# Layout of SBUF behind the value phase, Wq in a buffer of its own, and K's evacuation earlier in the step, in an attention and ternary-FFN kernel

## The reference

```python
q, k, v = proj(x, Wq), proj(x, Wk), proj(x, Wv)          # y = x @ W.T, split in 16 heads
scores = einsum('bhqd,bhkd->bhqk', q * min(cond, 4), k) / sqrt(64)
attn = softmax(where(causal, scores, min_float))
y = einsum('bhqk,bhkd->bhqd', attn, v) -> (8, 512, 1024) @ Wo.T
q_w = clip(round(w / alpha), -1, 1) * alpha               # alpha = mean |w|
q_x = clip(round(y / s), -128, 127) * s                   # s = row maximum / 127
out = x + q_x @ q_w.T + bias
```

## Time and profile before

| | |
|---|---|
| median of 3 runs | 2042.46 us (2041.6 to 2043.03) |
| profiled execution | 2044.32 us, its span 2042.3 us |
| granted TensorE clock, mean | 0.987 of full speed |
| TensorE / weight loads busy | 95% / 83% |
| VectorE / ScalarE / GpSimd busy | 66% / 50% / 45% |
| moved by DMA | 477.83 MB, mean 234 GB/s |
| chain that ended last | PE 82%, DVE 7%, DMA 4%, issue 3%, ACT 2%, POOL 2% |

### The profile page before, as it was taken

The page is one execution under the profiler, slowest core; times in us unless marked ns, Lnnn a source line. Parts: engine busy times, 40 slices in busy tenths (PEclk is TensorE's granted clock), DMA queues, the critical chain, the costliest instruction groups (busy, mean ns, idle before and its releaser), DMA issues.

```text
span 2042.3 us, 40256 instructions
## 1 busy us (share of the span) xinstructions
PE 1935.3 (95%) x12347; PEld 1697.0 (83%) x12378; DVE 1357.6 (66%) x3330; ACT 1027.5 (50%) x2495; POOL 916.2 (45%) x985
## 2 busy tenths in 40 slices
PE   8999889899998999998999999999988999999998
PEld 6788667899998999998999988999976777777775
DVE  6545665477778777788777787777777545454554
ACT  4443333377677776777777777777774000000000
POOL 1333443344446444465444455444454544444441
PEclk9999989899999999999999999999999999999999
DMA  6899998877777867777778777786772332323332
GB/s 216 327 374 350 343 344 313 300 270 242 271 267 264 284 246 269 275 254 260 274 261 287 233 273 261 256 286 236 277 242 76 118 110 92 123 92 116 100 101 73
DMA packets 165696, 477.83 MB, mean 234 GB/s; under 512 B 12768, under 2 KB 84448, under 8 KB 135776
## 3 DMA queue, kind: packets, MB, share of 16 engines
q1 hardware_dynamic: 165072, 476.11, 66.5%
q10 hardware_dynamic: 528, 0.52, 0.1%
HBM read 331.88 MB, written 111.15 MB: 217 GB/s over the span
## 4 chain that ended last, share of the span: by engine, by line
PE 82%; DVE 7%; DMA 4%; issue 3%; ACT 2%; POOL 2%; SPq 0%; DVEq 0%; ACTq 0%; POOLq 0%
PE proj_ps L211 26%; PE s_ps L598 9%; PE proj_ps L598 8%; PE o_ps L377 7%; PE t_ps L339 6%; PE t_ps L1012 6%; PE o_ps L669 5%; PE o_ps L1012 4%; PE s_ps L299 3%; PE s_ps L300 3%; DMA xv_raw<-xT 2%; DVE pt_all L363 2%; DMA parts<-x_scratch 2%; DVE prob L311 1%; DVE xv L910 1%
## 5 line engine op out<-in xcount | busy, mean ns | idle before, releaser
L211 PE MATMUL proj_ps<-parts 128*128 128x256 f32 x5376 | 770.2, 291 | 15.2 <-DMA parts<-x_scratch 10.0
L211 PEld LDWEIGHTS proj_ps<-parts 128*128 128x128 f32 x5376 | 678.5, 192 | 27.3 <-issue 10.5
L329 POOL TENSOR_TENSOR prob<-prob,row_inv 128x128 f32<-128x128 f32 (+3 forms) x512 | 376.9, 736 | 597.6 <-DVE row_inv L323 597.2
L317 ACT ACTIVATE prob<-prob,row_min 128x128 f32<-128x128 f32 (+3 forms) x512 | 287.6, 562 | 175.1 <-DVE row_min L311 167.8
L363 DVE TENSOR_TENSOR pt_all<-t_ps,pt_all 128x128 fp32r<-128x128 f32 (+3 forms) x512 | 249.4, 487 | 108.0 <-ACT pt_all L356 106.8
L339 PE MATMUL t_ps<-ident,prob 128*128 128x128 f32 x1280 | 229.3, 277 | 49.4 <-DVE pt_all L363 42.0
L311 DVE CUSTOM_DVE_ANT_0 prob<-s_ps,mask 128x128 f32<-128x128 f32 (+3 forms) x512 | 247.8, 484 | 34.1 <-PE s_ps L300 6.9
L654 ACT ACTIVATE yt_q<-t_ps 128x1024 bf16<-128x1024 bf16 x32 | 32.8, 1024 | 426.6 <-PE t_ps L647 426.6
L356 ACT ACTIVATE pt_all<-t_ps 128x128 fp32r<-128x128 f32 (+3 forms) x512 | 217.1, 424 | 8.5 <-PE t_ps L339 6.1
L339 PEld LDWEIGHTS t_ps<-ident,prob 128*128 128x128 f32 x1280 | 153.2, 142 | 72.4 <-issue 47.7
L598 PE MATMUL proj_ps<-wo_parts,o_parts 128*128 128x512 f32 x768 | 187.5, 398 | 0.0
(11 more groups left out here) (126 smaller groups left out, 2824.2 us busy)
## 6 DMA issues: line engine op xcount, KB each, us to landing
parts<-x_scratch SPq DMA_DIRECT2D x224, 1024.0 KB, 7.9
x_scratch<-xv SPq DMA_DIRECT2D x112, 512.0 KB, 5.9
k_sw<-k_st SPq DMA_DIRECT2D x128, 256.0 KB, 3.7
xv_raw<-xT SPq DMA_DIRECT2D x17, 1024.0 KB, 8.8
v_scratch<-v_tmp SPq DMA_DIRECT2D x64, 256.0 KB, 5.3
v_raw<-v_scratch SPq DMA_DIRECT2D x32, 512.0 KB, 3.9
oT_scratch<-o_sum SPq DMA_DIRECT2D x64, 256.0 KB, 2.6
o_raw<-oT_scratch SPq DMA_DIRECT2D x32, 512.0 KB, 4.6
```

The lines of the kernel that those rows point to most:

```text
L211: mm = pe.matmul(qk_bank(w, m), wc[w][:, c, wp, k, :], xq[:, c, :, xp, k, :], start=(fresh and k == 0 and i == 0), stop=(k == CH - 1 and i ...
L317: act.activation(prob[u % QT], prob[u % QT], ACT.Exp, bias=row_min[:, u % 4:u % 4 + 1], scale=-1.0, accum_out=row_sum[:, u % 4:u % 4 + 1]) ...
L329: pool.tensor_tensor(prob[u % QT], prob[u % QT], row_inv[:, u % 4:u % 4 + 1].broadcast_to([P, w]), ALU.mult).then_inc(norm_done, 1)
```

## The change

Five things are changed, and the arithmetic stays the same.

1. `parts` is laid out as x, Q's weights, K's weights instead of K, x, Q. Parts of x of batch 0 therefore lie on value weights that are free earlier in the last pair, K's weights on those that are free last. The buffers of the last phase and of the attention phase are put in another order.
2. The first Wq gets a buffer of its own, `w_first`, and is loaded in pair 2, right behind the first Wk. All later weights use `w_raw` as before.
3. In the last pair, SP issues all parts of x of batch 0 in the first four places. ScalarE and VectorE split two weights of K before the end of the pair and five behind it, and GpSimd forms the sums S1 and S3 one pair earlier, S2 and S4 behind the last one.
4. In the first step (no `old`), K's block 0 is evacuated right after K's last copy, and SP exchanges it ahead of the next batch's loads of x. ScalarE's wait for all stores of V moves with it.
5. In all steps with an `old`, VectorE makes K's low parts of block 0 ahead of L(6) instead of behind M(10).

```diff
-        parts = sb("parts", [P, 2 * WS + XS], F32R, p_ctx)
-        wc = [parts[:, i:i + WS]... for i in (0, WS + XS)]
-        xq = parts[:, WS:WS + XS]...
+        parts = sb("parts", [P, XS + 2 * WS], F32R, p_ctx)
+        xq = parts[:, 0:XS]...
+        wc = [parts[:, i:i + WS]... for i in (XS + WS, XS)]
...
+        w_all = [sb("w_raw", [P, KT * EG + CH * P], F32)]
+        w_all.append(sb("w_first", [P, KT * EG + CH * P], F32, wf_ctx))
@@ load_xq
-                sp.wait_ge(v_product_done, V_LAST + (3, 3, 4, 4, 5, 5, 6)[c])
+                sp.wait_ge(v_product_done, V_LAST + (1, 1, 2, 2, 3, 3, 4)[c])
@@ w_place, load_w
+        def w_place(n):
+            return 1 if n == 1 else 0
-            if n >= 1:
+            if n >= 2:
                 sp.wait_ge(qk_lo_done, 7 * n)
@@ split_w
-                    eng.wait_ge(v_product_done, V_LAST + (1 if c < 4 else 2))
+                    eng.wait_ge(v_product_done, V_LAST + (6 if c < 3 else 7))
@@ v_sp, last pair
-                        if m == 4:
-                            load_w(sp, 1)
-                        if m >= 2:
-                            for k in ((), (), (0, 1), (2,), (3, 4), (5,), (6,))[m]:
-                                load_xq(sp, 0, 0, k)
+                        for k in ((0,), (1, 2), (3, 4), (5, 6), (), (), ())[m]:
+                            load_xq(sp, 0, 0, k)
@@ v_sp, pair 2
                     load_w(sp, 0)
+                    load_w(sp, 1)
@@ v_act (v_dve alike, with True)
                 xv_next(act, n, 0, False)
-                if n == PAIRS - 1:
-                    for m in range(7):
-                        split_w(act, 0, m, False)
...
+                if n == PAIRS - 1:
+                    for m in range(2):
+                        split_w(act, 0, m, False)
                 v_copy(act, n, V_TMP_P)
                 xv_next(act, n, 6, False)
+            for m in range(2, 7):
+                split_w(act, 0, m, False)
@@ v_pool
-                if n == PAIRS - 1:
-                    for c in (S1, S3, S2, S4):
-                        w_sum(pool, 0, c)
                 v_ur(pool, n)
+                if n == PAIRS - 2:
+                    w_sum(pool, 0, S1)
+                    w_sum(pool, 0, S3)
+            w_sum(pool, 0, S2)
+            w_sum(pool, 0, S4)
@@ act_step
             copy(now, K, COPY_C21)
+            if now and not old:
+                for slot in v_stored:
+                    act.wait_ge(slot, PAIRS * 16)
+                evacuate(now, K, 0)
...
             copy(now, Q, COPY_U)
-            if now and not old:
-                for slot in v_stored:
-                    act.wait_ge(slot, PAIRS * 16)
-            evacuate(now, K, 0)
+            if old:
+                evacuate(now, K, 0)
@@ dve_step
             add(K, ADD_C12)
+            if not old:
+                evacuate(now, K, 0)
...
             W(11)
+            if old:
+                evacuate(now, K, 0)
             L(6)
             I(9)
             M(10)
-            evacuate(now, K, 0)
@@ sp_step
                 load_v(sp, *now)
+            if now and not old:
+                swap_k(sp, now[0], 0)
...
-            if now:
+            if now and old:
                 swap_k(sp, now[0], 0)
```

More of the change, by code:

```diff
@@ L78, in adaln_ffn_kernel @@
         p_ctx = ExitStack()
-        parts = sb("parts", [P, 2 * WS + XS], F32R, p_ctx)
-        wc = [parts[:, i:i + WS].rearrange("p (c a k e) -> p c a k e", c=7, a=2, k=CH) for i in (0, WS + XS)]
-        xq = parts[:, WS:WS + XS].rearrange("p (c j a k s) -> p c j a k s", c=7, j=2, a=2, k=CH)
+        parts = sb("parts", [P, XS + 2 * WS], F32R, p_ctx)
+        xq = parts[:, 0:XS].rearrange("p (c j a k s) -> p c j a k s", c=7, j=2, a=2, k=CH)
+        wc = [parts[:, i:i + WS].rearrange("p (c a k e) -> p c a k e", c=7, a=2, k=CH) for i in (XS + WS, XS)]
         p_ctx.close()
-        o_raw_all = sb("o_raw", [P, 2 * D], F32)
-        o_parts = sb("o_parts", [P, 2, 2, D], F32R)
-        y_q_all = sb("y_q", [P, 2, D], BF16)
         wo_ctx = ExitStack()
@@ L93, in adaln_ffn_kernel @@
         y_int = sb("y_int", [P, D], F32)
+        o_raw_all = sb("o_raw", [P, 2 * D], F32)
+        o_parts = sb("o_parts", [P, 2, 2, D], F32R)
+        y_q_all = sb("y_q", [P, 2, D], BF16)
         wo_hi, wo_lo = [[wo_parts[:, k, i, :] for k in range(KT)] for i in range(2)]
@@ L106, in adaln_ffn_kernel @@
         wf_out = [wf_mem[:, 2 * D + i * D // 2:2 * D + (i + 1) * D // 2].bitcast(BF16) for i in range(2)]
+        w_all.append(sb("w_first", [P, KT * EG + CH * P], F32, wf_ctx))
         wf_ctx.close()
+        w_raw = [w[:, 0:KT * EG].rearrange("p (k e) -> p k e", e=EG) for w in w_all]
+        w_extra = [w[:, KT * EG:].rearrange("p (k e) -> p k e", e=P) for w in w_all]
         one_ctx = ExitStack()
[L110 to L116, removed]
         PT_KEYS = 3 * P
@@ L121, in adaln_ffn_kernel @@
         pt_hi, pt_lo = [0, PT], [2 * PT, 3 * PT]
+        qk_sum = [sb(f"{n}_sum", [P, 2, S], F32, one_ctx) for n in "kq"]
+        qk_tmp = [sb(f"qk_{n}", [P, S // 2], F32, one_ctx) for n in "aur"]
+        v_raw = sb("v_raw", [P, QT, HG, DH], F32, one_ctx)
+        o_sum = [sb(f"o_sum{i}", [P, S], F32, one_ctx) for i in range(NBLK)]
+        k_st = sb("k_st", [P, HG, S], F32R, one_ctx)
+        k_sw = sb("k_sw", [P, HG, S], F32R, one_ctx)
+        q_st = sb("q_st", [P, HG, S], F32R, one_ctx)
+        v_st = sb("v_st", [P, QT, HG, 2 * DH], F32R, one_ctx)
         prob = [sb(f"prob{i}", [P, (i + 1) * P], F32, one_ctx)[:, :] for i in range(QT)]
-        o_sum = [sb(f"o_sum{i}", [P, S], F32, one_ctx) for i in range(NBLK)]
         one_ctx.close()
@@ L478, in split_w @@
             c, w, g = ORDER[m], n % 2, n // 2
-            src = {A11: w_quad(0, 0), A12: w_quad(0, 1), A22: w_quad(1, 1),
-                   S1: w_extra, S2: w_quad(0, 0), S3: w_quad(1, 0), S4: w_quad(0, 1)}[c]
+            src = {A11: w_quad(n, 0, 0), A12: w_quad(n, 0, 1), A22: w_quad(n, 1, 1),
+                   S1: w_extra[w_place(n)], S2: w_quad(n, 0, 0), S3: w_quad(n, 1, 0), S4: w_quad(n, 0, 1)}[c]
             if low:
@@ L1263, in v_dve @@
                     batch_scale(dve, 0, 0)
-                    for m in range(3):
-                        split_w(dve, 0, m, True)
                 v_sum(dve, n, 0)
-                if n == PAIRS - 1:
-                    for m in range(3, 7):
-                        split_w(dve, 0, m, True)
                 xv_next(dve, n, 2, True)
@@ L1279, in v_dve @@
                 wf_ternary(dve, n - WF_FROM, 1)
+                if n == PAIRS - 1:
+                    for m in range(2):
+                        split_w(dve, 0, m, True)
                 v_sum(dve, n, 3)
```

17 lines of the change are left out of this document (7 added, 10 removed).

## The result

The changed kernel takes 2010.48 us (median of four runs, 2008.18 to 2010.95) where the kernel before takes 2042.74 us in the same rounds (2041.6 to 2046.93): ratio 0.9836, 95% interval 0.9819 to 0.9853, 32.3 us less. The forecast was 2011.3 us. The profiled execution took 2008.18 us with a span of 2006.4, so the spans of the two profiled executions differ by 35.9 us. The granted clock was 0.991 on average, 0.987 before.

A forecast was written before the change was run, and what follows sets the result against it. TensorE, busy 95% of the span, was taken as the bound, gaining only where it waits. 20.2 + 1.5 + 2.1 + 1.2 + 6.5 - 0.3 = 31.2 us, from 2042.46 to 2011.3 us; range 2005 to 2022.

The forecast's parts named there:

- Part 1: Steps with an older one: K's low parts ahead of L(6) remove T(9)'s wait, 20.2 us in 24 regular steps, plus others.
- the regular steps: 24 attention steps: the whole wait before T(9) goes, 20.2 us together, at least nothing if T(8) takes it over.
- The K weight steps: Three steps preparing K's new weights: 0.5 us each, 1.5 us together (0 to 2.7), depending on GpSimd's lock.
- the Q weight steps: Three steps preparing Q's weights: the wait for L483 shortens, 0.7 us each, 2.1 us together (0 to 3.9).
- rival A: Regular steps: T(8) becomes late because L(6) slips 0.4 us more, costing 7.2 us, total 2018.5 us; chance 0.12.
- the last projecting step: Last step with projections, wait of 2.21 us: L(7) comes earlier, gaining 1.2 us (0 to 1.4).
- Part 2: Value phase's end and first step: earlier x, later K weights, next x's stream ending earlier; 6.5 us (3 to 9).
- One sign of the prediction: Second step: its last DMA wait was to end at about 392, where the stream had ended at 398.4.
- The second half of part 2: First step: K's products end at 360, so the next x's first load goes at 363.9, 5.5 us earlier than before.
- Rival B: First step gives nothing, total 2017.8 us, chance 0.10; held against it: 2.9 MB fewer ahead of x's last part.
- the start: Pair 2 and first step together: 6.5 us gained less 0.3 us lost, parts 2 and 3 of the forecast.
- Part 3: Pair 2 of the value phase: Wq's extra 1 MB load is mostly absorbed, loss 0.3 us (0 to 2.5).

The follow-up runs named there:

- the changed kernel's second trace: The changed kernel run again unedited, as yardstick beside experiments 7, 8 and 9: 2008.2 us, ratio 0.9834 to the kernel before.
- experiment 1: Kernel before with only VectorE's order changed, K's two low parts ahead of L(6) in steps with an older one: 2015.95 us, ratio 0.9841.
- experiment 3: Changed kernel with the first step's K evacuated and exchanged where it was before: 2012.06 us, ratio 0.9827 to the kernel before.
- experiment 6: Changed kernel with VectorE's C11 adds of K and Q ahead of the low split before each, first step only: 2010.0 us, ratio 0.9830.
- experiment 2: Changed kernel with VectorE's old order put back in the full steps, low parts behind M(10): 2043.9 us, ratio 0.9990 to the kernel before.
- Experiment 5: Changed kernel with GpSimd's first two sums of Wq formed one pair earlier, in the value phase: 2007.4 us, ratio 0.9808 to the kernel before.
- experiment 8: Changed kernel with GpSimd's first split of V behind N(8), where VectorE forms K's low parts: 2021.47 us, ratio 0.9883 to the kernel before.
- experiment 4: Changed kernel with the seven loads of the first x issued as late as before: 2012.44 us, ratio 0.9845 to the kernel before.
- experiment 7: Changed kernel with the next Wk's 1 MB load behind the next x's last two parts in the first step: 2006.12 us, ratio 0.9813.
- Experiment 9: Changed kernel with the edits of experiments 5, 6 and 7 together: 2001.04 us, ratio 0.9788 to the kernel before.

## Why the prediction was right, and where it was not

**Part 1 was right in mechanism, and a little small.** T(9)'s waits went, T(8)'s slack of 0.1 us held (L(6) ends at 980.81, T(8) starts at 981.10), the pair still takes 1.40 us. The size was off mainly for one reason: a row in brackets names less than a wait costs. Before, T(8) to the product with V was 1002.60 - 999.05 = 3.55 us, with 0.70 idle in it; after it is 983.78 - 981.10 = 2.68. The wait cost 0.87, 0.17 more than its row, about the 0.15 us by which matmul rows overlap each other. 24 times 0.17 is 4.1 us; the regular steps gave 3.3 us more than forecast. The K weight steps gave 0.9 each and not 0.5, the Q weight steps 1.0 each where 0.7 was taken, and the middle one 1.8 more: its wait for L483 had been 1.98 us and not 1.62, and the clock was low behind it (last section). In the K weight steps T(8) waits for 0.30 us now, of the kind of rival A:

```profile
621.88 0.30 PE L340 MATMUL t_ps<-ident,prob 128*128 128x128 f32 x1 [0.30 <-DVE pt_all L364]
```

In the last projecting step 1.2 us was forecast for a wait of 2.21. The transpose behind it comes 2.2 us earlier in this trace (counted from the step's first product with V), but 1.1 in the changed kernel's second trace and in those of experiments 1, 3 and 6, as forecast, and 0.8 in experiment 2, which has the old order. Another 1.0 us of the table's 3.2 falls in a stretch in which the clock was low for longer in before (0.80 in 1521.6 to 1536.6) than in after (0.89 in 1487.7 to 1501.7); in experiment 1 it was low further on as well (0.81 in 1514.7 to 1520.7, where before has 1.00), and its whole step is only 0.4 us shorter than before. So this row of the table is no measure of VectorE's order; what sets it stays open.

**Part 2 failed at one step**: "Two are ready at about 348, the third needs GpSimd's sum, and five splits (3.1 us) now stand ahead of ScalarE's first copy, which so ends at about 352.5. TensorE does two products until 351.0, waits 1.5, and does five more at 1.46 until 360." Five splits were priced on ScalarE, and that term was good: its copy ended at 353.4 and TensorE waited 1.16 us for it. On VectorE, where the low halves are made and which the prediction gave no time at this place, they took 5.88 us, because GpSimd formed Wq's sums beside them, with Wq in a buffer of its own and so ready; a sixth low split and then the add came behind. TensorE waited another 2.81, and K's products ended near 365 instead of 360 (high parts from 365.60); the value phase's end, 1.2 us later in this trace, is in that too. Experiment 5 shows the cause by taking it away. I had weighed the same lock for the regular and the weight steps, not for the first. Everything after it slipped. K's pair of low parts met GpSimd's splits of V and took 2.24 us instead of 1.40 (from 366.25), and the loads of the next x went from 369.73 instead of 363.9. One sign of the prediction came true all the same and says little: a wait for x ends at 392.75, near the 392 that was named. It is the sixth part's, which had ended at 394.12 before. The Trainium skill, SBUF — State Buffer, Who interferes with whom, has such VectorE and GpSimd instructions exclude each other for the whole instruction; the 5.88 against 3.70 us of experiment 5 and the 1.86 against 1.40 of experiment 8 agree.

The second half of part 2, loads of the next x 5.5 us earlier than before, rested on K's products ending at 360 and fell with it; experiment 3 shows that the place of the exchange did not matter to the time. The 2.9 MB that the prediction holds against rival B are not in the queue: between the parts of x it shows Wq's 1 MB and three stores of V of 256 KB, 1.75 MB. Rival B (the start gives nothing) was nearly the case for the start, at a total that its own price, 2017.8, did not meet, because part 1 was worth more.

**Part 3**: 0.3 us was forecast for Wq's load in pair 2. The gap at 85 us grew from 1.40 to 1.62, but it is 1.31 in the changed kernel's second trace. The value phase ended at 348.06 in before and 349.34 in experiment 1, without this load, and between 346.83 and 350.26 in the eight traces (the changed kernel's two and experiments 2, 3, 4, 6, 7 and 8) that have the load and the sums where the change has them. So the price is below what these traces can tell, within the forecast's bounds.

**How much the start really gave** depends on the trace, for that reason. From the first row of the projections to the first product with V (TensorE's timeline) it is 57.3 us in before and 59.0 in experiment 1; 55.4, 54.5, 55.8 and 55.7 in the changed kernel, in its second profile and in experiments 2 and 8; 55.9 in 3 and in 6, 56.7 in 4; 49.6 in 5, 50.7 in 7, and 45.8 in 9. By this measure the change gave 1.5 to 4.5 us at the start, with which the 2 us of experiment 2 agree; the 0.75 of the two profiled executions is this less 1.2 us by which the value phase of one ended later.

**So two errors cancelled**: the start was 4 us too large (6.2 against the 2.0 of experiment 2), the steps some 7 us too small. By the table these are 3.3 in the regular, 1.2 in the K and 2.7 in the Q weight steps; by experiment 1, VectorE's order alone gave 1.59%, 32.5 us (29 to 36), where 25.0 was forecast. That the forecast hit by less than a microsecond is luck; these pieces alone would put the gain at 34, and the measured ratio's interval (30 to 37 us) holds both. The range and the chances rested on the mechanism of part 1, which held.

## What to carry to other kernels

When a load is made early so that its data no longer waits, list all work that this data releases on every engine: here GpSimd's sums started at once and slowed the splits that had become the critical ones. Price a chain of splits on the engine that ends last, and with what runs beside it. Time that an idle row names can be less than was lost (0.69 to 0.91 for 0.85 to 1.05 us per regular step, 4.9 for 10.5 in experiment 8): compare the period from start to start of the same row in two steps. And before a difference of 1 to 3 us between two traces is given to an edit, look at the same stretch in every other trace that has the edit.

## What the runs showed of the hardware

Behind some waits TensorE's rows show a lower granted clock, so that such a wait costs more than itself. The clearest case is a regular place with and without the wait. In the middle one of the Q weight steps of before, TensorE waits 1.98 us; six projection products right behind it take 1.63 us, where they take 0.96 in the same place of the other two:

```profile
963.73 0.97 PE L211 MATMUL proj_ps<-parts 128*128 128x256 f32 x6 [1.98 <-DVE parts L483]
...
965.12 1.63 PE L211 MATMUL proj_ps<-parts 128*128 128x256 f32 x6
```

The clock was 0.71 in 965 to 970 and 1.00 behind the waits of 1.62 us in the other two steps. That step takes 38.26 us and they take 36.38 and 36.41. Experiment 2, the other trace with the old order, repeats it (wait 1.98, clock 0.67 in 963 to 968, step 38.28). In the ten traces with the new order the wait at this place is 0.30 us, and the step takes 35.3 to 35.4 us.

The waits of the first step show the same, less cleanly. After (stretches: length, busy times of the engines, clock, DMA share, GB/s), where TensorE had waited 2.81 us before 358 and 3.35 us before 393 (the rows behind the second one take 1.62 us again for six products):

```profile
355.00:365.00 10.00, 7.19 (x50) 7.05 (x49) 7.67 (x10) 2.44 (x5) 2.96 (x4) 0.83 0.61 208
...
390.00:395.00 5.00, 2.25 (x11) 2.28 (x12) 0.25 (x2) 1.17 (x3) 2.34 (x3) 0.67 0.99 291
395.00:400.00 5.00, 5.00 (x31) 4.92 (x30) 3.46 (x10) 1.78 (x6) 0.40 (x1) 0.65 0.59 151
```

Experiment 9, whose longest wait there is 1.16 us, has full clock in the same stretches:

```profile
355.00:365.00 10.00, 9.64 (x78) 9.24 (x77) 6.35 (x10) 5.28 (x11) 4.42 (x5) 1.00 0.61 201
...
390.00:395.00 5.00, 4.63 (x35) 4.21 (x34) 3.02 (x12) 2.35 (x7) 2.16 (x3) 1.00 1.07 322
395.00:400.00 5.00, 5.00 (x42) 4.83 (x41) 3.70 (x11) 4.45 (x12) 2.26 (x4) 1.00 0.94 338
```

The two levels are 1.2 and 2.4 GHz (0.5 and 1.00); values between them are read as stretches that hold some of each. In the kernel before it was 0.66 in 355 to 365, behind the wait for x of 5.23 us. Experiment 7 took 2.9 us off the waits for x (6.3 to 3.4), and its way from the projections to the first product with V is 3.8 us shorter than that of the changed kernel beside it, with a clock of 1.00 in 390 to 395 where this has 0.66: the rest may be the clock. In experiment 5 the wait for k_sum is 2.2 us shorter, the way 4.9 us shorter than in the changed kernel's second trace, and the clock in 355 to 365 is 1.00 for 0.83. No run separates a wait of the start from the clock behind it.

GpSimd and VectorE share the loss when they meet: in experiment 8 VectorE's pair lost 0.46 us to 1.35 us of GpSimd's work, nearly all of it in its second instruction (1.12 for 0.68), and GpSimd's second took 1.07 for 0.74. The first of the pair took 0.71 although 0.16 us of GpSimd's first lay beside it. In the first step, where GpSimd's instructions are longer, VectorE's two that met them took 1.76 and 1.78 us for 0.68, and GpSimd's 1.72 and 1.74 for 1.30.
